# Second attention: the place of the residual addition in VectorE's step

## The reference, cut to what matters

```python
s1 = jnp.where(allowed, q1 @ k1.T * scale, NEG)      # q, k split into two halves of 64
s2 = jnp.where(allowed, q2 @ k2.T * scale, NEG)
a1, a2 = softmax(s1), softmax(s2)
diff = relu(a1 - lam * a2)
diff = diff / (diff.sum(-1) + 1e-6)
out = diff @ v                                       # 16 heads, head size 128
x = x + out @ Wo                                     # and the experts' output
```

## Time and profile before

| | us |
|---|---|
| median of 3 runs | 2958.39 (2957.83 to 2962.09) |
| the profiled execution, its own time | 2956.44 |
| its span, first to last instruction | 2954.3 |
| TensorE busy | 2577.7 (87% of the span) |
| VectorE busy | 1724.0 (58%) |
| ScalarE, GpSimd busy | 1080.1 (37%), 1014.0 (34%) |
| mean granted TensorE clock | 0.949 |
| heads blocks of the second attention | from about 1490 to 1869 and from about 1935 to 2326 in the span |

### The profile page before, as it was taken

How to read it: one execution, slowest core, us unless ns; L and a number is a source line. 1 busy time by engine, 2 the same in 40 slices (tenths; PEclk the granted TensorE clock), 3 DMA queues, 4 the chain that set the end, 5 groups by cost and what they waited for, 6 DMA issues and landing times. The chain is left out here.

```text
span 2954.3 us, 35819 instructions
## 1 busy us (share of the span) xinstructions
PE 2577.7 (87%) x12276; PEld 1739.3 (59%) x12276; DVE 1724.0 (58%) x4042; ACT 1080.1 (37%) x2539; POOL 1014.0 (34%) x748
## 2 busy tenths in 40 slices
PE   5889898989599999994689998879998677699998
PEld 2334444434288888882567776657776433387776
DVE  4557676765155555546478887458888311156664
ACT  1125454445233333222156666146666211111211
POOL 2318676767311121100056665034444100123330
PEclk9969999999799999997899999999999898899999
DMA  7361212110200000001121000000000599610001
GB/s 259 125 142 28 56 23 51 22 40 1 100 15 15 14 14 28 0 1 62 36 74 36 22 26 12 15 29 8 8 15 1 194 380 357 204 53 20 15 8 57
DMA packets 158052, 189.41 MB, mean 64 GB/s; under 512 B 51406, under 2 KB 105678, under 8 KB 157504
## 3 DMA queue, kind: packets, MB, share of 16 engines
q1 hardware_dynamic: 131776, 147.43, 16.1%
q10 hardware_dynamic: 14592, 27.27, 2.9%
q0 software_dynamic: 11520, 12.64, 1.3%
HBM read 159.85 MB, written 52.43 MB: 72 GB/s over the span
## 5 line engine op out<-in xcount | busy, mean ns | idle before, releaser
L588 DVE TENSOR_REDUCE mx<-bank 128x1 f32<-128x512 f32 x512 | 326.4, 678 | 125.5 <-PE bank L495 121.4
L435 POOL TENSOR_TENSOR probs<-probs 128x1024 f32<-128x1024 f32 x128 | 301.4, 2375 | 211.9 <-PE bank L518 174.9
L646 ACT ACTIVATE probs<-bank 128x1024 f32<-128x1024 f32 x256 | 250.2, 1022 | 274.3 <-PE bank L508 274.3
L822 POOL TENSOR_TENSOR up_lo<-up_raw,up_hi 128x1024 fp32r<-128x1024 f32 (+1 forms) x28 | 74.9, 2695 | 719.2 <-ACT up_hi L812 719.2
L1450 POOL TENSOR_SCALAR mix<-mix,sm 128x256 f32<-128x256 f32 (+1 forms) x256 | 228.7, 904 | 225.5 <-DVE sm L1347 225.3
L1390 ACT ACTIVATE ms<-ms,sm 128x256 f32<-128x256 f32 (+1 forms) x512 | 247.9, 487 | 133.8 <-DVE sm L1318 130.8
L892 DVE TENSOR_TENSOR hid<-bank,sg 128x512 f32<-128x512 f32 x108 | 74.6, 691 | 317.0 <-ACT sg L842 309.7
L842 ACT ACTIVATE sg<-bank 128x512 f32<-128x512 f32 x108 | 64.6, 598 | 482.1 <-PE bank L768 482.0
L495 PE MATMUL bank<-k_parts,q_parts 96*128 96x512 f32 x512 | 216.9, 475 | 10.1 <-DVE mx L588 4.5
L495 PEld LDWEIGHTS bank<-k_parts,q_parts 96*128 96x128 f32 x512 | 93.8, 195 | 171.4 <-DVE mx L588 139.0
L1318 DVE CUSTOM_DVE_ANT_0 ms<-bank,misc 128x256 f32<-128x256 f32 (+1 forms) x512 | 183.9, 397 | 0.1
(11 more groups left out here) (199 smaller groups left out, 5565.8 us busy)
## 6 DMA issues: line engine op xcount, KB each, us to landing
ewg<-in_L_ffn_Wg_dram SPq DMA_DIRECT2D x32, 704.0 KB, 13.2
ewu<-in_L_ffn_Wu_dram SPq DMA_DIRECT2D x32, 704.0 KB, 15.6
ewd<-in_L_ffn_Wd_dram ACTq DMA_DIRECT2D x32, 512.0 KB, 11.5
q_parts<-qk_dram SPq DMA_DIRECT2D x48, 256.0 KB, 4.4
up_raw<-in_L_ffn_W_dram SPq DMA_DIRECT2D x16, 512.0 KB, 4.5
ewd<-in_L_ffn_Wd_dram ACTq DMA_DIRECT2D x32, 192.0 KB, 14.9
qk_dram<-qk_hi SPq DMA_DIRECT2D x4, 1280.0 KB, 5.2
qk_dram<-qk_lo SPq DMA_DIRECT2D x4, 1280.0 KB, 7.2
```

The lines of the kernel that those rows point to most:

```text
L435: pool.tensor_tensor(probs[:, even, half, :], probs[:, even, half, :], probs[:, odd, half, :], ALU.add).then_inc(S["paired"], 1)
L588: dve.reduce_max(mx[:, U % 2, q, h:h + 1], bank[:, h, :], AX.X).then_inc(S["max"], 1)
L646: act.activation(probs[:, s % BUFS, 2 * x:2 * x + 2, :], bank[:, 2 + 2 * x:4 + 2 * x, :], ACT.Exp, scale=scale).then_inc(S["exps"], 1)
```

## The change

In VectorE's loop, the two lines that call `add(s - 5)` move from behind `combine(s-1)` to right behind `mask(s, 1)`. So in a step the addition now stands ahead of `values_low(s-4)`, of `output_low` and of `combine(s-1)`. No operation, wait or buffer is added or taken away, and the other engines' queues stay as they are.

```diff
             if s < UNITS:
                 mask(s, 1)
+            if s >= 5:
+                add(s - 5)
             if 4 <= s < UNITS + 4:
                 values_low(s - 4)
             if s % NT == 4 and s < UNITS:
                 output_low(s // NT)
             if 1 <= s <= UNITS:
                 combine(s - 1)
-            if s >= 5:
-                add(s - 5)
             if s // 4 + AHEAD < CHUNKS and s % 2:
                 turn_queries(s // 4 + AHEAD, s % 4 // 2)
```

## The result

The changed kernel takes 2896.28 us (median of 6 runs, 2894.04 to 2900.24) against 2960.4 before on the same occasions (6 runs, 2957.83 to 2965.36): a ratio of 0.9784, 95% interval 0.9772 to 0.9797. That is 64 us less; 46 were forecast, and the range ended at 2908. The direction and the place were right, the size was not, and nearly the whole error turns out to be one reading of the trace.

The account below looks back on a forecast made before the run. TensorE was taken as the bound, idle only before the output projection. Twice 21.7 us a half (16.4 + 5.6 - 0.3) gave 43.4, plus 3.0 for the clock 46.4: forecast 2912.0 us, 8-in-10 range 2908 to 2926.

Parts of the forecast that it names:

- What bounds the kernel: Steps 4 to 55: TensorE bounds, with holes only before the output projection; a step without a hole is 5.54 us.
- (a): Steps 4 to 55: nearly all waits of the output projection for the addition go, 16.4 us in a half.
- The replay of step 12: Step 12 with the addition moved: the low part comes 0.3 us early and the projection follows `weigh` without a hole.
- rival 1: After each rotation `weigh` waits 0.3 to 0.6 us for the low part: 12 us, time 2924; chance 0.23.
- (b): Steps 56 to 64: steps repeat every 5.0 us instead of 5.53, a gain of 5.6 us in a half.
- (c): Steps 65 to 68: the addition delays the low part, the last projection comes later; minus 0.3 us in a half.
- (d): TensorE's clock: both falls behind the long holes go, a gain of 3.0 us; bounds 0 and a loss of 3.
- (2): Additions collide with GpSimd's `normalise`, making `weigh` late in 26 steps: 21 us, time 2933; chance 0.04.
- (3): Loop of projection, addition, low part and `weigh`, 3.85 us long, binds as VectorE waits for `y`: 2989; chance 0.04.
- Rival 4: The time stays at 2958, since TensorE's holes fill with a wait for ScalarE's copy; chance 0.03.

Follow-up runs that it names:

- experiment 1: Against the kernel before: the addition moved inside the combination, between its two last operations; 2929.24 us, ratio 0.9904.
- experiment 2: Kernel before plus one small VectorE operation between combination and addition, in steps 5 to 64 of both halves; 2969.38 us, ratio 1.0039.
- Experiment 4: Changed kernel, but the addition stays behind the combination in steps 20, 36 and 52 of both halves; 2908.32 us, ratio 0.9829.
- experiment 6: Changed kernel with the low part ahead of the addition, both ahead of the combination; 2891.11 us the first time, 2894.22 us the second.
- experiment 3: Changed kernel plus one small VectorE operation behind the combination, with the addition already done; 2894.59 us, ratio 0.9788.
- experiment 5: Changed kernel below step 56, the addition at its old place from step 56 on; 2908.66 us, ratio 0.983.

## Why the prediction was wrong in size, point by point
**What bounds the kernel.** "TensorE, and its only holes are those in front of the output projection" was right as to the place. "A step without a hole ... 5.54 us of pure work" was wrong, and it is the step that failed. Steps without a bracket were taken to be at their floor. All but six in each half were held by the addition as well, by 0.20, as experiments 1 and 2 show.
"VectorE is late as a whole" in the steps after a rotation was right too, but `turn_queries` is not all of it. The first operation of `invert` (L1344, two elements in each row) takes 0.15 to 0.16 us in 100 of 128 cases. In the other 28, steps 4, 8, 12 and so on to 56 of both halves, it starts while GpSimd works on the rotation, takes 0.81 to 1.14, and ends 0.01 to 0.02 us behind GpSimd's operation. In step 12 of the kernel before:

```profile
1556.40 1.30 POOL L1443 TENSOR_TENSOR q<-tr 128x512 f32<-128x512 f32 x1 [3.78 <-DVE tr L1310]
...
1556.85 0.87 DVE L1344 SCALAR_TENSOR_TENSOR sm<-sm 128x2 f32<-128x2 f32 x1
```

The 0.72 us that it takes too long are most of that step's hole (0.73 of idle time and 0.24 hidden). The changed kernel has the same 28 cases, 0.82 to 1.14 us, but most of the delay is off TensorE's path. No experiment took the rotation away, so the hold is read from these rows alone.

**(a), steps 4 to 55.** Predicted 16.4, and 1.5 for the clock, in a half; measured 293.3 - 268.0 = 25.3. The visible waits did go, all 16.5 of them. The term for what a hole costs beyond its idle time was taken as 0.04 for 22 holes, 0.8. By the distance from `weigh` to L1282 it is 0.24 in those 22 steps, 0.20 in 23 steps that showed no hole, and nothing in the six steps of 5.34: 10.1 in a half. The 0.04 came from a comparison of a step with a visible hole and one with a hidden one, so the hidden one cancelled. Against it, new waits that the prediction had put at 0.9 are: 0.5 in steps 8, 24 and 40, 0.25 in steps 20, 36 and 52, 0.09 in steps 12, 28 and 44, 2.5 together. 16.5 + 10.1 - 2.5 + 1.5 = 25.6 for the measured 25.3.
The replay of step 12 was off by little: the low part was to be 0.3 early, and step 12 has a hole of 0.09. In steps 8, 24 and 40, which the prediction did not replay, it left up to 0.28 of idle time. This is rival 1, in 3 steps of a half instead of 13. The 0.25 at steps 20, 36 and 52 was put at 0.3, where the low output weights end last. The profile gives no bracket there, but in all six L1282 starts 0.05 behind the end of L1356, and so it does in step 4 of both halves of both kernels: they are what releases it, as forecast.

**(b) and (c), steps 56 on.** Predicted 5.3 in a half; measured 57.4 - 51.2 = 6.2. The steps were to repeat every 5.0 us and do so every 4.9, since L1282 starts 0.91 behind `weigh` there and not 1.01 to 1.05. The last projection came 0.24 later for the low part (1.11 of idle time for 0.87), for 0.3 predicted.

**(d), the clock.** Taken as gone, 3.0 us, and it is gone: 1.00 in the whole stretch of both halves. The trace of before bears the size out: the granted clock was 0.50 from 1608.00 to 1611.00 and from 2065.10 to 2068.40, behind the first long hole of each half, and step 21 of the two halves took 7.07 and 7.12 us for the 5.54 of step 22, 1.5 and 1.6 more. That both falls would go with the holes was the author's estimate. Experiment 4 brings one fall back with six holes, so falls go with the holes, though not with each.

**The rivals.** The collision of the addition with GpSimd (2) did not come: the 128 additions take 680 to 690 ns beside its runs, 673 to 690 before. What GpSimd does hold is the small operation of `invert`, shown above. The loop through `y` (3) closed in the last steps alone. VectorE waits for `y` 20.4 us in 28 cases: by 0.25 in 18 cases below step 56, where `weigh` is not late for it, and for the rest from step 64 on. In steps 64 to 66 `weigh` starts 0.15 behind the low part, which stands behind the addition, and 0.13 behind ScalarE's copy; that it is the low part that holds it shows in steps 56 to 62, where the distance to the copy is 0.05. The profile names the copy in all of them. A turn of this loop takes 3.74 to 3.75 us, for 3.85 in the prediction; steps 65 and 66 took 3.68 before. With the last projection it costs 0.36 in a half (term (c) had 0.3), and it is gone when the low part comes first, as in experiment 6. Rival 4 fell.

**The range.** It ended at 2908 with the words that there were no waits left to remove. That bound was made of the profile's idle time alone. The holes that a modelled end can cover needed a bound of their own, one for each step: 102 steps below 56, and each up to the 0.24 by which the end of `weigh` overlaps the next start.

## What to carry to other kernels
Whether an instruction waits for another is not told by its idle time but by the distance from the releaser's end to its start: if that is the same in every step, the wait is there, whatever the bracket says. The distance to look for is not one number: here it is 0.15 for the last semaphore that an instruction waits for (the addition, or the low part ahead of `weigh`) and 0.05 for one waited for before it (the copy ahead of `weigh`, the low weights). That the order of the waits decides this is read from these cases, not tested. Before calling a step's length the floor of its engine, find the smallest start-to-start distance of each piece over all steps (step 9 had it), or delay the suspected releaser by a known small amount and see whether the step follows, as in experiment 2. And in a queue written out by hand, put what another engine waits for ahead of what waits for that engine.

## What the runs showed of the hardware
- Behind the eight matmuls of 128x128x128 of `weigh`, the next group started 0.81 us after their start in the six steps of each half that took 5.34 us before the change (step 9, for one) and in the steps of 5.34 after it, while the profile gives the eight 1.05 us. So a wait of up to 1.05 - 0.81 = 0.24 us shows no idle time there; in the steps of 5.54 one of 0.20 showed none.
- The granted clock fell to 0.50 for 3.4 us behind holes of 1.6 to 2.0 us (in the kernel before 0.50 from 1608.00 to 1611.00, with TensorE busy for 3.00 of 3.00 us). In the profiles of the four kernels that keep such holes (24 of them: before, experiments 1, 2 and 4) it fell behind 8. A ninth fall, in experiment 2, came behind a hole of 1.06 us in step 56 of the second half (granted clock 0.62 from 2280.00 to 2284.50). Behind the 136 holes of 0.15 to 1.00 us before the output projection in these four profiles there was none. In the six profiles without the long holes (the changed kernel twice, experiments 3 and 5, experiment 6 twice) it never fell within the steps. Each fall cost 1.4 to 1.6 us: steps of 6.87 to 7.17 for 5.34 to 5.62.
- A small VectorE operation (L1344) that started while GpSimd's L1443 ran ended 0.01 to 0.02 us behind it: 28 of 128 cases before and 28 after, 0.81 to 1.14 us for 0.15 to 0.16.
- A VectorE operation of two elements in each row (L1380, experiment 2) takes 0.15 us in the profile, but the next one started 0.07 to 0.08 behind its start, where nothing waited between them.
